# Toeplitz blocks of the FIR filters loaded as two bands of 32 columns

## The chip, the cores and the metric

One core of one Trainium2 chip. The metric is the device time of one execution in microseconds (us). The kernel before has a median of 714.42 us over 3 runs (714.11 to 716.6).

## The reference

A token mixer and a feed-forward layer over `x` of 4 x 1024 x 256, all float32. The mixer adds, per head and token, a chunked delta rule (a scan over chunks), the values `v` themselves and three causal filters along the tokens (FIR) of `v`; five gates weight them:

```
FIR_S, FIR_M, FIR_L = (3, 15, 63)
local_s = _fir(v_direct, fir_s)      # depthwise: each of the 256 channels has its own taps
local_m = _fir(v_direct, fir_m)
local_l = _fir(v_direct, fir_l)
o = probs[..., 0:1] * local_s + probs[..., 1:2] * local_m + probs[..., 2:3] * local_l
    + probs[..., 3:4] * delta_out + probs[..., 4:5] * v_direct
```

Then a norm, an output product, a layer norm, and the feed-forward part. The change touches only how the filters reach the chip.

## The kernel before, in words

The kernel runs in three stages, and each engine's program is written out in order by hand, with semaphores between engines.

**Stage A (to about 103 us)**: per batch row `b`, VectorE (DVE) takes row statistics (`a_row_stats`), normalises with `a_norm` (line 1030, a tensor_scalar from SBUF to SBUF) and does the short convolution of `v` (`a_conv`, line 1042). TensorE (PE) transposes and multiplies, ScalarE (ACT) copies out of PSUM. GpSimd (POOL) has in this stage only the small powers of `a_power` (line 487) and, behind the powers of `b` = 0 and of `b` = 1, a memset on the filter blocks (line 493). The values end in `vwin`, with 128 token offsets on the partitions.

**FIR stage (to about 177 us)**: a filter is applied as a product with a Toeplitz block: for each channel, 128 window rows by 64 output tokens. The host lays the blocks out (`padded`). Output token t of the 63-tap filter needs window rows 2+t to 64+t, that of the 15-tap filter rows 50+t to 64+t; the rest of a block is zeros. Channels come in 16 groups of 16. One group is one `load(g)` on the sync engine's DMA queue (SP): line 281 brings the long filter (`fl`), line 282 the two short ones (`fms`, rows 48 to 127 only, the rows above having been zeroed by the memset). Four buffers (NB = 4) rotate: `toep_in(g)` waits until PE is through with group g - 4 and then issues `load(g)`. Groups 0 to 3 load during stage A. Between `toep_in(5)` and `toep_in(6)` SP writes and reads back a small tensor (`beta`, lines 402 and 404), and behind `toep_in(11)` it issues the first two windows of the next stage (`window_in`, line 323, four transfers).

PE works in tiles of four channels (`fir_tile(q)`, 64 tiles, a group is four tiles). Two tiles (a pair) are 16 MATMUL records at line 1541, two at a time side by side on the two column halves, and behind each pair come two transposes of an earlier pair (line 1550). DVE multiplies each tile by the gates (line 1134), POOL adds the three filters (lines 502 and 504).

**Stage C (to the end)**: the projections (line 1611), the triangular solve on POOL (lines 571 and 573), the scan and the feed-forward part. PE's first projection stands behind its last FIR tile in program order, and its bank is free only after that.

Of the kernel before, what the change touches and what calls it, by code (L numbers as in the profile page):

```python
# [36 lines left out]
P = 128  # L37
B, L, D, H = 4, 1024, 256, 4
DK = D // H
C = 64  # L40
# [7 lines left out]
PAD = TAPS - 1  # L48
LP = L + PAD
NG = 6  # L50
MS0 = 48
ROWS = 2 * P - C

LEAD = 8
RING = LEAD + 1
# [6 lines left out]
GC = 16  # L62
NB = 4
NF = 3
TILES = D // 4
PER = GC // 4
ROW = NF * C
FPAIRS = 2
FG = D // GC
# [10 lines left out]
def build(nc, x, out, wgate, consts, smalls, wq, wk, wv, wo, wr, wfk, wfv, fl, fms):  # L80
    ctx = ExitStack()
    with ctx:
        def sb(name, shape):
            return ctx.enter_context(nc.sbuf_tensor(name, shape, F32))
# [17 lines left out]
        w = {k: sb("w_" + k, [P, HALVES, D]) for k in ("q", "k", "v", "o", "r", "fk", "fv")}  # L102
# [20 lines left out]
        A_V = BLK * D  # L123
        A_T = NB * NF * C * GC
        arena = sb("arena", [P, A_V + A_T])
        vwin = arena[:, 0:A_V].rearrange("p (c w) -> p c w", w=BLK)
        toep = arena[:, A_V:A_V + A_T].rearrange("p (i f c t) -> p i f c t", i=NB, f=NF, c=GC)

        def carve(whole, at, *shape):
            n = 1  # L130
# [34 lines left out]
        for i in range(RING):  # L165
            whole, at = (arena, low) if i < 3 else (seq, rest_) if i < EARLY else (arena, high)
            kq.append(carve(whole, at, 2 * U, C).rearrange("p (u i) t -> p u i t", i=2))
        for i in range(RING):
            whole, at = (cva.rearrange("p a t -> p (a t)"), [0]) if i == 0 else (arena, low) if i == 1 else (seq, rest_) if i < 5 else (arena, high)
# [28 lines left out]
        bank = [ctx.enter_context(nc.psum_tensor(f"bank{i}", [P, 512], F32)) for i in range(8)]  # L198
# [22 lines left out]
        HH = [slice(0, 64), slice(64, 128)]  # L221
# [26 lines left out]
        def fir_bank(q):  # L248

            return q % 4 if q < TILES // 2 else (3, 6, 7)[(q - TILES // 2) % 3]  # L250
# [9 lines left out]
        def _(sp):  # L260
# [17 lines left out]


            def load(g):  # L280
                sp.dma_start(toep[:, g % NB, 0], fl[g]).then_inc(s[f"toep{g % NB}_in"], 16)
                sp.dma_start(toep[MS0:P, g % NB, 1:3], fms[g]).then_inc(s[f"toep{g % NB}_in"], 16)


            v_dst = v_dram.rearrange("(n two) t r b k -> two t r b n k", two=2)
# [12 lines left out]
            for b in range(B):  # L298
                if b + 2 < B:
                    rows_of(b + 2, 0)  # L300
                    rows_of(b + 2, 1)
                xT_store(b)
                if b < 2:
                    sp.wait_ge(s["toep_zero"], b + 1)
                    load(2 * b)
                    load(2 * b + 1)
                v_store(b)


            def toep_in(g):  # L310
                sp.wait_ge(s["fir_mm"], (g - NB + 1) * PER)
                load(g)
# [84 lines left out]
            for pr in range(PAIRS):  # L397
                for q in range(4):
                    hh, half = divmod(q, 2)
# [76 lines left out]
        def _(pool):  # L476
# [8 lines left out]
            def a_power(b, h):  # L485
                pool.wait_ge(s["a_stats"], 6 * b + 3 * h + 3)
                pool.tensor_tensor(rs_a[:, 4 * h:4 * h + 4], ve_a[:, 4 * h:4 * h + 4], neg_half[:, 0:4], ALU.pow).then_inc(s["a_rs"], 1)

            for b in range(B):
                for h in range(2):  # L490
                    a_power(b, h)
                if b < 2:
                    pool.memset(toep[0:MS0, 2 * b:2 * b + 2, 1:NF], 0.0).then_inc(s["toep_zero"], 1)


            def fir_sum(h):
# [936 lines left out]
        def _(pe):  # L1433
            mm = nc.tensor.matmul
# [88 lines left out]
            def fir_tile(q):  # L1523

                g, pr, dp = q // PER, q // (TILES // 2), q % (TILES // 2)
                if q % PER == 0:
                    pe.wait_ge(s[f"toep{g % NB}_in"], 32 * (g // NB + 1))
                if q >= TILES // 2 + 3:
                    pe.wait_ge(s["fir_prod"], q - 2)
                elif q > TILES // 2:  # L1530
                    pe.wait_ge(s["beta_T"], PAIRS)
                elif q == TILES // 2:
                    pe.wait_ge(s["fir_prod"], TILES // 2)
                elif q >= 4:
                    pe.wait_ge(s["fir_prod"], q - 3)
                out_ = bank[fir_bank(q)][:, 0:2 * ROW].rearrange("p (f w) -> p f w", f=NF)
                for hh in range(2):
                    for i in range(2):
                        d = 2 * dp + i
                        cin = (GC // 2) * hh + d % (GC // 2)  # L1540
                        last = mm(out_[HH[i], :, 64 * hh:64 * hh + C], vwin[:, P * pr + 64 * hh + d, :],  # L1541
                                  toep[:, g % NB, :, cin, :], start=True, stop=True)
                last.then_inc(s["fir_mm"], 1)

            def fir_turn(q):
# [22 lines left out]
            for h in range(HALF_PAIRS):  # L1568
                if h == 1:
                    fir_gates(0)  # L1570
                    fir_gates(1)
                if h == 4:
                    beta_turn()
                fir_tile(2 * h)
                fir_tile(2 * h + 1)
                if h >= 2:
                    fir_turn(2 * (h - 2))
                    fir_turn(2 * (h - 2) + 1)

            def fir_tiles(n, i):  # L1580
                fir_tile(2 * late_pair(n, i))
                fir_tile(2 * late_pair(n, i) + 1)
# [353 lines left out]
```

## Time and profile before

| | |
|---|---|
| median of 3 runs | 714.42 us |
| profiled execution, its own time | 716.96 us |
| its span, first to last instruction | 715.0 us |
| mean granted TensorE clock | 0.915 |
| PE busy / DVE busy / POOL busy | 79% / 68% / 57% |
| bytes moved by DMA | 63.44 MB |
| `arena<-fl`: x16, each | 512.0 KB |
| `arena<-fms`: x16, each | 640.0 KB |

The profiled execution is 2.5 us above the median of the timed runs, and 1.96 us of it lie outside the span. A busy share is an average over three stages with different limits; what an edit is worth is read from the stage it is in.

### The profile page before, as it was taken

The numbers are of one execution on the slowest core, as the hardware profiler recorded it, in microseconds if no ns is written. First come the engines' busy times: TensorE is split into PE (matmuls) and PEld (weight loads), VectorE is DVE, ScalarE is ACT, GpSimd is POOL, SyncE is SP. The second block draws the span as 40 slices with busy tenths as digits, with TensorE's granted clock in tenths as the row PEclk, the third lists the DMA queues.
The fourth block names the chain that finished last, engine by engine and source line by source line (L and its number), as shares of the span: only waits on it lengthen the run. The fifth ranks groups of instructions, "written<-read, shape, count | busy, mean of one in ns | idle before, by whom it ended". The sixth has DMA issues, their size and how long they took to land.

```text
span 715.0 us, 20289 instructions
## 1 busy us (share of the span) xinstructions
PE 567.2 (79%) x7980; PEld 454.8 (64%) x7980; DVE 482.9 (68%) x1166; ACT 283.0 (40%) x703; POOL 406.4 (57%) x503
## 2 busy tenths in 40 slices
PE   3788769768687676578989989989867678999964
PEld 2566546545574465467877878768766567788853
DVE  6999755434646353178798796797864666788863
ACT  2688831111535244043444443634513223444421
POOL 3211018546100298548998457899649999666522
PEclk9999979999979696699999998999989898999987
DMA  8749447995112610543213243031251111422201
GB/s 279 202 137 256 154 126 195 236 224 114 31 32 56 64 47 17 92 66 74 50 25 93 54 89 71 19 86 47 68 87 31 42 46 35 84 62 57 55 15 29
DMA packets 111149, 63.44 MB, mean 89 GB/s; under 512 B 81744, under 2 KB 104144, under 8 KB 109776
## 3 DMA queue, kind: packets, MB, share of 16 engines
q1 hardware_dynamic: 111056, 62.16, 37.6%
q8 instruction: 63, 1.03, 0.6%
q14 instruction: 30, 0.25, 0.1%
HBM read 43.18 MB, written 18.95 MB: 87 GB/s over the span
## 4 chain that ended last, share of the span: by engine, by line
DVE 26%; POOL 25%; PE 17%; issue 12%; DMA 11%; SPq 7%; ACT 2%; POOLq 0%; DVEq 0%; ACTq 0%
POOL seq L573 7%; DMA arena<-fms 6%; POOL seq L571 6%; POOL arena L582 5%; DVE arena L1160 5%; DVE cva L1042 4%; DVE arena L1257 3%; SPq L367 3%; PE bank L1729 3%; PE bank L1541 2%; PE bank L1611 2%; PE bank L1645 2%; POOL arena L544 2%; POOL arena L594 2%; DVE arena L1245 2%
## 5 line engine op out<-in xcount | busy, mean ns | idle before, releaser
L1160 DVE SCALAR_TENSOR_TENSOR arena<-bank,small,arena 128x256 f32<-128x256 f32 x192 | 91.4, 482 | 25.7 <-ACT arena L816 20.8
L582 POOL TENSOR_TENSOR arena<-arena,neg_half 128x2 f32<-128x2 f32 (+1 forms) x64 | 61.5, 961 | 74.2 <-DVE arena L1252 54.3
L573 POOL TENSOR_TENSOR seq<-seq 128x31 f32<-128x31 f32 (+15 forms) x124 | 86.7, 699 | 9.7
L571 POOL TENSOR_TENSOR seq<-seq 128x31 f32<-128x31 f32 (+15 forms) x124 | 69.4, 560 | 7.9
L1541 PE MATMUL bank<-arena 128*64 128x192 f32 x512 | 51.4, 345 | 16.9 <-DMA arena<-fms 13.3
L1134 DVE TENSOR_TENSOR seq<-bank,seq 128x384 f32<-128x384 f32 x64 | 35.2, 557 | 43.4 <-PE bank L1541 33.2
L502 POOL TENSOR_TENSOR seq<-seq 128x256 f32<-128x256 f32 x32 | 23.2, 726 | 68.0 <-DVE seq L1134 63.0
L816 ACT ACTIVATE arena<-bank,small 128x256 f32<-128x256 f32 x64 | 30.4, 475 | 58.6 <-PE bank L1611 58.5
L528 POOL TENSOR_TENSOR arena<-seq,powers 128x16 f32<-128x16 f32 x16 | 47.3, 2956 | 10.7 <-DVE seq L1169 10.7
L1541 PEld LDWEIGHTS bank<-arena 128*64 128x64 f32 x512 | 35.5, 142 | 27.5 <-DMA arena<-fms 15.7
L1611 PE MATMUL bank<-arena,w_q 128*128 128x268 f32 x128 | 37.5, 429 | 15.0 <-DVE arena L1160 14.9
L1611 PE MATMUL bank<-arena,w_k 128*128 128x268 f32 x128 | 40.6, 457 | 7.1 <-DMA arena<-xnT_scratch 6.6
L1042 DVE SCALAR_TENSOR_TENSOR cva<-bank,small,cva 128x256 f32<-128x256 f32 x96 | 39.9, 476 | 6.8 <-ACT cva L695 6.5
L1257 DVE TENSOR_SCALAR arena<-arena 128x256 f32<-128x256 f32 x64 | 30.3, 514 | 16.9 <-POOL arena L582 16.9
L1611 PEld LDWEIGHTS bank<-arena,w_q 128*128 128x128 f32 x128 | 23.9, 202 | 27.5 <-DVE arena L1160 23.9
L1729 PE MATMUL bank<-w_o,arena 128*128 128x256 f32 x128 | 36.2, 432 | 1.5 <-ACT arena L870 1.4
L1729 PE MATMUL bank<-w_fv,seq 128*128 128x256 f32 x128 | 36.5, 435 | 0.8 <-ACT arena L901 0.8
L553 POOL MEMSET seq<- 128x1024 f32 x4 | 3.8, 950 | 57.8 <-DVE seq L1194 57.8
L1295 DVE SCALAR_TENSOR_TENSOR seq<-seq,small,arena 128x256 f32<-128x256 f32 x64 | 35.5, 596 | 0.3
L1611 PEld LDWEIGHTS bank<-arena,w_k 128*128 128x128 f32 x128 | 26.2, 218 | 14.8 <-DMA arena<-xnT_scratch 7.0
L1622 PE MATMUL bank<-cst,arena 64*64 64x4 f32 x1024 | 34.3, 200 | 0.2 <-DVE arena L1160 0.2
L1729 PE MATMUL bank<-w_r,seq 128*128 128x256 f32 x128 | 33.2, 404 | 1.5 <-DVE seq L1295 1.5
(159 smaller groups left out, 1422.3 us busy)
## 6 DMA issues: line engine op xcount, KB each, us to landing
arena<-fms SPq DMA_DIRECT2D x16, 640.0 KB, 13.4
arena<-fl SPq DMA_DIRECT2D x16, 512.0 KB, 10.9
arena<-xnT_scratch SPq DMA_DIRECT2D x32, 134.0 KB, 2.8
gram_scratch<-arena SPq DMA_DIRECT2D x16, 256.0 KB, 2.3
arena<-v_scratch SPq DMA_DIRECT2D x32, 128.0 KB, 3.1
arena<-x SPq DMA_DIRECT2D x64, 64.0 KB, 2.2
out<-arena SPq DMA_DIRECT2D x64, 64.0 KB, 2.1
xnT_scratch<-seq SPq DMA_DIRECT2D x2, 1027.0 KB, 8.5
```

Source lines behind the costliest of these rows:

```text
L528: pool.tensor_tensor(rk, ssel[:, slot_of(n)], powers[:, :, :], ALU.pow).then_inc(s["norms"], 1)
L571: pool.tensor_tensor(part, below, above, ALU.mult).then_inc(s["solve"], 1)
L573: last = pool.tensor_tensor(into, into, part, ALU.add)
L582: pool.tensor_tensor(dst, src, half8 if k == U else neg_half[:, 0:k], ALU.pow).then_inc(s[dst_sem], 1)
L1042: nc.vector.scalar_tensor_tensor(cva[:, i, :], bank[2 + i][:, j:j + 256], conv_w[:, 2, i, j:j + 1], cva[:, i, :], ALU.mult, ALU.add).then_ ...
L1134: nc.vector.tensor_tensor(fprod[:, q % (2 * FPAIRS), :], bank[fir_bank(q)][:, 0:2 * ROW], fgate[:, q // (TILES // 2), :], ALU.mult).then_i ...
L1160: nc.vector.scalar_tensor_tensor(cv[:, t], ps[:, :, j:j + C], conv_w[:, 1 - t // 2, t % 2, j:j + 1], cv[:, t], ALU.mult, ALU.add).then_inc ...
L1257: last = nc.vector.tensor_scalar(dst[:, j, :], src[:, j, :], mv[:, i, j, 0:1], rs[:, i, j:j + 1], ALU.subtract, ALU.mult)
L1295: nc.vector.scalar_tensor_tensor(dst[:, hf].rearrange("p (b t) -> p b t", b=B), dx[:, hf].rearrange("p (b t) -> p b t", b=B), mu[:, i, hf: ...
L1541: last = mm(out_[HH[i], :, 64 * hh:64 * hh + C], vwin[:, P * pr + 64 * hh + d, :], toep[:, g % NB, :, cin, :], start=True, stop=True)
L1611: last = mm(bank[g][:, 0:B * (C + PAD)], w["kq"[kind]][:, kh, P * g:P * g + P], xwin4[:, m % 2, kh], start=(kh == 0), stop=(kh == 1))
L1729: last = mm(dst[:, 256 * j:256 * j + 256], lhs[:, kh, P * j:P * j + P], wt[:, kh, :], start=(kh == 0), stop=(kh == 1))
```

## The change

A block of 64 columns is cut into two bands of 32 columns. Band 0 of the long filter has its taps in rows 0 to 95, band 1 in rows 32 to 127; the short ones in rows 48 to 95 and 80 to 127. Only these rows are loaded: `load(g)` has four transfers, two of 96 rows with 2 KB each (192 KB) and two of 48 rows with 4 KB each (192 KB). The memset now covers all 128 rows and all three filters of two buffers at once. In SBUF a buffer is laid out band, filter, channel, column; the matmul's moving operand is read in six runs of 32 columns in place of three of 64 (still 192), and its output access pattern puts them where they stood before.

```diff
-MS0 = 48
+BAND = C // 2
+LONG, SHORT = (0, 96), (48, 96)
...
-        toep = arena[:, A_V:A_V + A_T].rearrange("p (i f c t) -> p i f c t", i=NB, f=NF, c=GC)
+        toep = arena[:, A_V:A_V + A_T].rearrange("p (i s f c t) -> p i s f c t", i=NB, s=2, f=NF, c=GC)
...
             def load(g):
-                sp.dma_start(toep[:, g % NB, 0], fl[g]).then_inc(s[f"toep{g % NB}_in"], 16)
-                sp.dma_start(toep[MS0:P, g % NB, 1:3], fms[g]).then_inc(s[f"toep{g % NB}_in"], 16)
+                for h in range(2):
+                    sp.dma_start(toep[BAND * h + LONG[0]:BAND * h + LONG[1], g % NB, h, 0], fl[g, h]).then_inc(s[f"toep{g % NB}_in"], 16)
+                    sp.dma_start(toep[BAND * h + SHORT[0]:BAND * h + SHORT[1], g % NB, h, 1:3], fms[g, h]).then_inc(
+                        s[f"toep{g % NB}_in"], 16)
...
-                    pool.memset(toep[0:MS0, 2 * b:2 * b + 2, 1:NF], 0.0).then_inc(s["toep_zero"], 1)
+                    pool.memset(toep[:, 2 * b:2 * b + 2], 0.0).then_inc(s["toep_zero"], 1)
...
-                    pe.wait_ge(s[f"toep{g % NB}_in"], 32 * (g // NB + 1))
+                    pe.wait_ge(s[f"toep{g % NB}_in"], 64 * (g // NB + 1))
...
-                out_ = bank[fir_bank(q)][:, 0:2 * ROW].rearrange("p (f w) -> p f w", f=NF)
+                out_ = bank[fir_bank(q)][:, 0:2 * ROW].rearrange("p (f k s t) -> p k s f t", f=NF, k=2, s=2)
...
-                        last = mm(out_[HH[i], :, 64 * hh:64 * hh + C], vwin[:, P * pr + 64 * hh + d, :],
-                                  toep[:, g % NB, :, cin, :], start=True, stop=True)
+                        last = mm(out_[HH[i], hh], vwin[:, P * pr + 64 * hh + d, :],
+                                  toep[:, g % NB, :, :, cin, :], start=True, stop=True)
...
-    def padded(f):
+    def padded(f, rows_of):
...
-        return rows.reshape(ROWS, FG, GC)[at].transpose(2, 0, 3, 1)
+        whole = rows.reshape(ROWS, FG, GC)[at].transpose(2, 0, 3, 1)
+        return np.stack([whole[:, BAND * h + rows_of[0]:BAND * h + rows_of[1], :, BAND * h:BAND * h + BAND] for h in range(2)], axis=1)
...
-        "fl": padded(g["attn_fir_l"]),
-        "fms": np.stack([padded(g["attn_fir_m"]), padded(g["attn_fir_s"])], axis=2)[:, MS0:],
+        "fl": padded(g["attn_fir_l"], LONG),
+        "fms": np.stack([padded(g["attn_fir_m"], SHORT), padded(g["attn_fir_s"], SHORT)], axis=3),
```

## Rows read from the trace of the kernel before

**Rows 1.** The page's second part: busy tenths of DMA in 40 slices.
```profile
DMA  8749447995112610543213243031251111422201
```

**Rows 2.** Chain that ended last, 88 to 182 us, shares by line.
```profile
by line: DMA arena<-fms 48.6%; PE bank L1541 18.8%; DMA v_scratch<-fir 4.7%; PE bank L1550 4.1%; SPq L295 2.4%; PE bank L1466 2.4%; PE bank L1611 2.3%; issue 1.9%; DVE cva L1042 1.8%; DVE seq L1134 1.7%; DVE arena L1160 1.6%; POOL seq L502 
```

**Rows 3.** Waits, 96 to 178 us: us in total, times, longest.
```profile
PE bank L1541 <- DMA arena<-fms: 13.3, 9, 3.3
```

**Rows 4.** Timeline of PE: start us, us, what, in brackets the idle time before.
```profile
119.47 1.52 PE L1541 MATMUL bank<-arena 128*64 128x192 f32 x16
...
121.29 1.52 PE L1541 MATMUL bank<-arena 128*64 128x192 f32 x16
...
156.84 2.72 PE L1541 MATMUL bank<-arena 128*64 128x192 f32 x16 [3.31 <-DMA arena<-fms]
...
173.23 1.52 PE L1541 MATMUL bank<-arena 128*64 128x192 f32 x16
```

**Rows 5.** The same chain in order of time: start us, us, what.
```profile
118.12 12.03 DMA arena<-fms
...
153.57 17.80 DMA arena<-fms
```

**Rows 6.** Timeline of SP's DMA issues: start us, us, what.
```profile
108.23 0.43 SPq L282 DMA_DIRECT2D arena<-fms  x1
...
115.86 0.50 SPq L281 DMA_DIRECT2D arena<-fl  x1
...
127.63 0.33 SPq L281 DMA_DIRECT2D arena<-fl  x1
128.00 0.43 SPq L282 DMA_DIRECT2D arena<-fms  x1
...
134.56 10.47 SPq L323 DMA_DIRECT2D arena<-xnT_scratch  x4
145.49 3.68 SPq L281 DMA_DIRECT2D arena<-fl  x1
```

**Rows 7.** DMA issues from 108.1 to 109 us, last column us to landing.
```profile
arena<-fms SPq DMA_DIRECT2D x1, 640.0 KB, 5.7
```

**Rows 8.** The same view from 127.9 to 128.5 us.
```profile
arena<-fms SPq DMA_DIRECT2D x1, 640.0 KB, 17.4
arena<-fl SPq DMA_DIRECT2D x1, 512.0 KB, 13.9
```

**Rows 9.** Windows: stretch, length, busy of PE, PEld, DVE, ACT, POOL, clock, DMA, GB/s.
```profile
4.50:9.00 4.50, 0.00 (x0) 0.00 (x0) 3.18 (x14) 0.21 (x1) 1.02 (x1) 1.00 1.04 316
...
119.00:134.50 15.50, 11.60 (x113) 7.76 (x110) 7.38 (x14) 2.36 (x4) 9.58 (x14) 1.00 1.03 239
```

**Rows 10.** Chain that ended last, 0 to 32 us, in order of time.
```profile
10.94 3.41 issue
...
24.82 1.64 DVE seq L1030 x2
```

**Rows 11.** Timeline of POOL, 0 to 32 us.
```profile
10.68 3.60 POOL L493 MEMSET arena<- 48x4096 f32 x1
17.41 1.01 POOL L487 TENSOR_TENSOR rs_a<-ve_a,neg_half 128x4 f32<-128x4 f32 x1 [3.12 <-DVE ve_a L1022]
...
22.64 3.50 POOL L493 MEMSET arena<- 48x4096 f32 x1
```

**Rows 12.** Line 553: duration ns min/median/max, first and last start, shape.
```profile
L553 POOL MEMSET seq<- x4: 942/952/957, 245.3 to 534.5; 128x1024 f32 x4
```

**Rows 13.** Line 1030 by itself, the same columns.
```profile
L1030 DVE TENSOR_SCALAR seq<-seq,mv_a,rs_a x16: 396/408/3530, 9.5 to 49.7; 128x256 f32<-128x256 f32 x16
L1030 DVE TENSOR_SCALAR seq<-fir,mv_a,rs_a x16: 394/404/1482, 24.8 to 67.5; 128x256 f32<-128x256 f32 x16
```

**Rows 14.** Matmuls of lines 1611 (four runs of 67 columns) and 1729 (one run).
```profile
L1611 PE MATMUL bank<-arena,w_k x128: 389/389/816, 177.3 to 498.8; 128*128 128x268 f32 x128
...
L1729 PE MATMUL bank<-w_o,arena x128: 379/379/796, 320.6 to 687.7; 128*128 128x256 f32 x128
```

## The prediction

> **What bounds the kernel now.** I read four views in this order. The page's slices show where DMA is nearly full: at the start, about 50 us, and in slices 7 to 9, roughly 120 to 175 us, which is the FIR stage [rows 1]. The chain of waits there names the transfer of the short filters for 48.6% of 94 us, and PE's own tiles for only 18.8% [rows 2]. PE stops nine times for it, 13.3 us in all, 3.3 at the longest [rows 3]. The timeline gives PE's own pace: pairs start at 119.47 and 121.29, so a pair costs 1.82 us, and a group (two pairs) 3.64. That is pair 10; pair 31, the last, starts at 173.23, where 119.47 + 21 x 1.82 = 157.69 would have done. So the stage is 15.54 us longer than PE needs, which includes one pair after the longest stall that ran at a lower clock, 2.72 in place of 1.52 us [rows 4]. After the stage PE's projections follow in program order and nothing in stage C waits for a clock of its own, so what is saved here moves the end by as much.
>
> **How fast the filters come.** The chain follows two transfers to their landing: group 7 at 118.12 + 12.03 = 130.15, group 15 at 153.57 + 17.80 = 171.37 [rows 5]. Between them lie eight groups of 1152 KB and two windows (four transfers of 134 KB, 536 KB): 9752 KB in 41.22 us, 4.23 ns per KB. A group costs 4.87 us against PE's 3.64, the windows 2.27. A group that meets an empty queue landed 5.7 us after its last issue [rows 6, 7], 0.4 after the first (two issues follow each other so, 127.63 and 128.00 [rows 6]): 6.1, of which 6.1 - 4.87 = 1.2 is fixed.
>
> **Part 1, fewer bytes.** 2 x 192 + 2 x 192 = 768 KB in place of 1152. By the byte a group costs 768 x 4.23 = 3.25 us, below PE's 3.64. Follow it with times as if nothing ahead had moved. Group 6 is issued at 115.86 [rows 6], held until then by the beta round trip; two more issues for group 5 lie ahead of that and add some 0.4: 116.2 + 1.2 + 3.25 = 120.7, and PE wants it at 123.11. Group 12 has six more groups and the windows ahead: 120.7 + 6 x 3.25 + 2.27 = 142.5, wanted at 119.47 + 14 x 1.82 = 144.95. Group 15: 152.2, wanted at 155.87. None is late, by 2.4 us at least, and the whole 15.5 comes back. In general group 15 lands at 119.7 + 10c, with c the time of a group, so PE waits from c = 3.62 on, and each 0.1 us on c costs 1 us.
>
> What c could be: the low end is 3.25 or less, no gain beyond the 15.5. Shorter rows do not speak against it: x in rows of 1 KB moved at 316 GB/s, the filters in rows of 4 and 8 KB at 239, at a full queue both times [rows 9]. The high end comes from group 9's followers: the long filter of group 10 landed at 127.63 + 13.9 = 141.5, the short ones at 128.00 + 17.4 = 145.4 [rows 6, 8]. That is 3.9 us for 640 KB in rows 48 to 127, so 6.1 ns per KB, while the long filter over all 128 rows had at most the remaining 1 us or so of that group's 4.87, 2 ns per KB. A transfer that sits mostly in the upper 64 rows is slow, or an engine of the queue has more of it. Bounded that way, the two short pieces (rows 48 to 95 and 80 to 127, all but 16 of 96 rows in the upper half) cost 192 x 6.1 = 1.17 each, 2.3 together; the two long ones (each two to one between the halves) cost between 0.8 and 2.3 together. So c is 3.1 to 4.65. Summed over the halves it is 256 KB below and 512 above, before 384 and 768: the same two to one, so if the pieces overlap, c is two thirds of 4.87 again. I take 3.25 to 3.7 as likely and charge 0.6 us for it.
>
> The Trainium skill bears on this: "SBUF — State Buffer", section on the DMA port swizzle, says a DMA's bandwidth goes by how many of 16 ports its partitions reach, partitions 0 to 63 all on eight of them and 64 to 127 on the other eight, and the section after it that two DMAs on the two halves do not add up. By its figure of 218 GB/s for eight ports the four pieces one after another would take about 0.6 + 0.6 + 0.6 + 0.9 = 2.7 us, an estimate from that page. The rate of 6.1 ns per KB above is in line with its direction, not with its size. Its direction makes the second rival below.
>
> **Part 2, SP's issues.** 32 more, 0.33 to 0.43 us each [rows 6], 1.7 us per group where a group has 3.64: hidden. In the middle SP stood 10.47 us at the windows and 3.68 at the next filter, since the queue was backed up [rows 6]. With the backlog gone by then to one or two groups, that wait ends when the windows begin to move, about 137, and group 12 is still issued in time. If it is not, group 12 is late by some 2 us; part of the 0.6 charge is for this.
>
> **Part 3, the larger memset.** Each memset grows from 4096 to 6144 elements per partition. POOL's two took 3.60 and 3.50 us with 48 partitions [rows 11]; one of 1024 elements on 128 took 0.95 [rows 12], so the slope is (3.55 - 0.95) / 3072 = 0.85 ns per element whatever the partitions, and each grows by 2048 x 0.85 = 1.74 us. POOL itself has the room (its next instruction is at 17.41 after 3.12 us idle [rows 11]), and SP's filter loads come later. But DVE does not. Its normalisation (line 1030) needs 0.4 us, and took 3.53 once and 1.48 once [rows 13]: the chain stands still for 3.41 us from 10.94, and for 1.64 at 24.82 for two of them [rows 10], in both cases until the memset is over (10.68 + 3.60 = 14.28; 22.64 + 3.50 = 26.14) [rows 11]. DVE is the chain there and runs on without a gap, so the first memset delays everything by 1.74. The second then starts as much later, meets the same instruction, and delays by 1.74 again. Together 3.5 us, on the path, since from there to the FIR stage DVE, ACT and PE wait only for one another. The ends: 0 if the wait were not for the memset, 3.5 if it is; two instructions that end with it make it 3.5.
>
> **Part 4, the matmul's pattern.** 192 columns as before, in six runs. Between four runs of 67 columns and one of 256 the median differs by 389 - 379 = 10 ns for 12 more columns [rows 14], 0.83 ns per column and nothing for the three added runs. At most the 10 ns are all runs: 10 ns on 8 steps of a pair, 30 pairs, 2.4 us. A gain is excluded, since columns are the same. I take 0.
>
> **Sum.** -15.5 + 0.6 + 3.5 = -11.4 us. The profiled span would be 703.6 and its execution 705.6; on the median of 714.4 that is 703.0. What is late next: in the FIR stage PE itself, at 1.82 us a pair.
>
> **Rivals.**
> A (forecast, 0.62): c up to 3.7, memset on the path: 702 to 704.5.
> B (0.17): the pieces cost more than the bytes say, c = 3.7 to 4.4, or SP's wait at the windows starves group 12. At c = 4.0 group 15 lands at 159.7, 3.8 us late: 714.4 - 15.5 + 3.8 + 3.5 = 706.2; at 4.4 it is 710. For it: the slow short filters [rows 8]. Against: the same two to one over the halves.
> C (other side, 0.07): transfers that cover half the height do not overlap, and all four run at 6.1 ns per KB: c = 768 x 6.1 = 4.7. Then the ten groups from 6 on save only 10 x (4.87 - 4.7) = 1.7 us, the memsets take 3.5: 716.2, slower. It decides from 10 x (4.87 - c) = 3.5, c about 4.5. Against it: it needs the long pieces, a third of whose rows are in the other half, to be as slow as the short ones.
> D (0.08): the longer memset does not hold DVE longer: 699.5. Against it: rows 10, 11 and 13 agree to 0.2 us.
> E (0.06): the change does its work, but matmuls in six runs or a lower clock in the denser stage cost 2 to 5 us: 705 to 708.
>
> **How the numbers follow.** Range 699.5 to 709: D and E in full, B but for its upper end, C left out. Below 0.5% (3.6 us), about what this kernel's runs can tell from nothing, lie only C and the last of B: faster 0.88, same 0.05, slower 0.07.
>
> **What would show it.** Both memsets at about 5.3 us, line 1030's longest instructions at about 5.3 and 3.2 us, and pair 10 starting at 123 in place of 119.47. Pairs every 1.82 us from there to the last, which starts near 161; no wait of line 1541 for `fms` over 1 us; SP's stall at the windows much shorter than 10.47. Landing times of a group's last piece below 10 us in the place of 17.4. The prediction is wrong if pairs come at over 1.85 us with no wait in between (part 4), if line 1541 still waits in every group (C), or if the FIR stage begins where it began (D).

## The result, and the profile after

| | kernel before | changed kernel |
|---|---|---|
| median of 17 executions | 717.57 us (714.02 to 1287.64) | 709.45 us (703.88 to 714.3) |
| ratio, 95% interval | | 0.9895 (0.986 to 0.993) |
| profiled execution, span | 715.0 us | 701.9 us |
| bytes moved | 63.44 MB | 57.15 MB |

The ratios here and below compare means over the executions that lie within 1.5% of the fastest of their kernel, which leaves out the one of 1287.64 us, and on the chip of memsets_moved_2 and both_moved_2 leaves only 8 of the 17 of the kernel before (mean 713.5 us, that of all 17 is 718.5).

By the ratio the kernel is faster by 7.5 us (5.0 to 10.0) where 11.4 was forecast, and 709.45 lies just outside the range that ended at 709. The single profiled execution, though, gained 13.1 us of span; it was the fastest of its 17. So there are two questions: did the steps go as worked out, and why do executions and profile differ?

The chain of waits from 88 to 182 us, shares by line, answers to [rows 2]:

```profile
by line: PE bank L1544 47.9%; PE bank L1553 11.7%; DMA v_scratch<-fir 5.2%; PE bank L1614 4.0%; DVE arena L1163 3.7%; PE bank L1648 3.1%; DVE gates L1101 2.5%; SPq L298 2.4%; PE bank L1469 2.4%; issue 2.3%; PE bank L1625 2.2%; DVE seq L1137
```

No filter transfer is left in it; PE's own tiles (line 1544, before 1541) are 47.9%. The timeline of PE, answering to [rows 4] (first the pairs 2 and 3, then 10, 15, 16 and 31):

```profile
108.21 2.15 PE L1544 MATMUL bank<-arena 128*64 128x192 f32 x16 [3.34 <-DVE seq L1137]
...
110.91 2.22 PE L1544 MATMUL bank<-arena 128*64 128x192 f32 x16
...
124.77 1.52 PE L1544 MATMUL bank<-arena 128*64 128x192 f32 x16
...
133.87 1.52 PE L1544 MATMUL bank<-arena 128*64 128x192 f32 x16
...
136.15 1.52 PE L1544 MATMUL bank<-arena 128*64 128x192 f32 x16 [0.38 <-DVE seq L1137]
...
163.45 1.52 PE L1544 MATMUL bank<-arena 128*64 128x192 f32 x16
```

Pairs come every 1.82 us in six runs as they did in three. Two things are new: pair 16 waits for DVE (its bank is the one that pair 15 used; before, the DMA wait covered that), and pairs 2 and 3 ran at a lower clock, 2.15 us in place of 1.52 (from 108.21 to 113.70 us the granted clock was 0.69).

Stage A: the chain from 0 to 32 us, POOL's memsets, and line 1033 (before 1030) by itself, answering to [rows 10, 11, 13]:

```profile
11.02 5.12 issue
...
27.59 1.68 DVE seq L1033
29.27 0.45 issue
```

```profile
10.76 5.31 POOL L496 MEMSET arena<- 128x6144 f32 x1
...
24.43 5.22 POOL L496 MEMSET arena<- 128x6144 f32 x1
```

```profile
L1033 DVE TENSOR_SCALAR seq<-seq,mv_a,rs_a x16: 394/406/5236, 9.5 to 53.2; 128x256 f32<-128x256 f32 x16
L1033 DVE TENSOR_SCALAR seq<-fir,mv_a,rs_a x16: 395/407/2203, 27.6 to 71.3; 128x256 f32<-128x256 f32 x16
```

The memsets take 5.31 and 5.22 us (5.3 forecast) and DVE is held for 5.12 in place of 3.41. The longest instruction of the first form is 5.24 us as forecast, that of the second 2.20 where 3.2 was.

How fast the filters come, at a full queue: SP's issues of the last pieces of groups 7, 11, 12, 13 and 15 at line 284, then their landing times in the same order, from the DMA issues at each of these times:

```profile
125.11 0.41 SPq L284 DMA_DIRECT2D arena<-fms  x1
...
136.72 1.46 SPq L284 DMA_DIRECT2D arena<-fms  x1
...
145.25 0.43 SPq L284 DMA_DIRECT2D arena<-fms  x1
...
147.13 0.43 SPq L284 DMA_DIRECT2D arena<-fms  x1
...
151.97 0.43 SPq L284 DMA_DIRECT2D arena<-fms  x1
```

```profile
arena<-fms SPq DMA_DIRECT2D x1, 192.0 KB, 5.6
...
arena<-fms SPq DMA_DIRECT2D x1, 192.0 KB, 7.9
...
arena<-fms SPq DMA_DIRECT2D x1, 192.0 KB, 5.4
...
arena<-fms SPq DMA_DIRECT2D x1, 192.0 KB, 6.8
...
arena<-fms SPq DMA_DIRECT2D x1, 192.0 KB, 8.1
```

Group 7 landed at 130.7 and group 11 at 144.6, so c was (144.6 - 130.7) / 4 = 3.5 us there. Behind the windows group 12 landed at 150.65, group 13 at 153.9 and group 15 at 160.1: c = (160.1 - 153.9) / 2 = 3.1 us, with the last group, which has nothing behind it, in the mean. 3.25 was forecast and 4.87 measured before. SP's stop at the windows is shorter (four issues 2.59 us in place of 10.47), the one at group 12 is not (3.26 us against 3.68):

```profile
138.38 2.59 SPq L326 DMA_DIRECT2D arena<-xnT_scratch  x4
141.01 3.26 SPq L283 DMA_DIRECT2D arena<-fl  x1
```

### The profile page after: what moved, and what is told of

Read it like the earlier page. It is cut to its first block, busy times and chain, and to the rows that moved or that the text cites. A ratio compares the mean times of both kernels' runs of the same rounds, so it can differ in the third digit from the quotient of the medians.

```text
span 701.9 us, 20321 instructions
## 1 busy us (share of the span) xinstructions
PE 572.8 (82%) x7980; PEld 458.1 (65%) x7980; DVE 486.5 (69%) x1166; ACT 282.6 (40%) x703; POOL 410.4 (58%) x503
## 2 busy tenths in 40 slices
DMA packets 112941, 57.15 MB, mean 81 GB/s; under 512 B 82256, under 2 KB 104656, under 8 KB 112848
## 4 chain that ended last, share of the span: by engine, by line
DVE 27%; POOL 25%; PE 24%; issue 13%; DMA 4%; SPq 4%; ACT 2%; POOLq 0%; DVEq 0%; ACTq 0%
POOL seq L576 7%; PE bank L1544 6%; DVE arena L1163 6%; POOL seq L574 6%; POOL arena L585 5%; DVE cva L1045 4%; PE bank L1732 4%; DVE arena L1260 3%; PE bank L1614 3%; PE bank L1648 2%; POOL arena L547 2%; SPq L370 2%; DVE seq L1298 2%; PE bank L1625 2%; PE bank L1457 2%
## 5 line engine op out<-in xcount | busy, mean ns | idle before, releaser
L505 POOL TENSOR_TENSOR seq<-seq 128x256 f32<-128x256 f32 x32 | 23.3, 729 | 54.3 <-DVE seq L1137 54.2
L1614 PE MATMUL bank<-arena,w_k 128*128 128x268 f32 x128 | 43.3, 482 | 6.5 <-DMA arena<-xnT_scratch 5.1
L1614 PEld LDWEIGHTS bank<-arena,w_k 128*128 128x128 f32 x128 | 27.8, 232 | 14.9 <-DMA arena<-xnT_scratch 5.5
L1625 PEld LDWEIGHTS bank<-cst,arena 64*64 64x64 f32 x1024 | 34.3, 145 | 1.9 <-issue 1.4
```

What stands on the lines that cost most here:

```text
L1614: last = mm(bank[g][:, 0:B * (C + PAD)], w["kq"[kind]][:, kh, P * g:P * g + P], xwin4[:, m % 2, kh], start=(kh == 0), stop=(kh == 1))
L1625: last = mm(bank[1][q, NONE * (U * kind + u):NONE * (U * kind + u) + NONE], sq[q, U * kind + u], ones[q], start=True, stop=True)
```

## The experiments

They ran with 6 or 12 timed executions each, on three chips, beside 17 of the kernel before on the same chip. Stage times come from one profile each: "FIR" is from the start of pair 2 to that of pair 31 in PE's timeline, "gap" from pair 31 to the first memset of the solve, the first work of POOL in stage C.

| kernel | ratio (95%) | pair 0 | FIR | pair 31 | gap | span |
|---|---|---|---|---|---|---|
| before, first profile | | 95.65 | 69.28 | 173.23 | 72.1 | 715.0 |
| changed, first profile | 0.9895 (0.986-0.993) | 99.44 | 55.24 | 163.45 | 69.5 | 701.9 |
| after_again | 0.9866 (0.9819-0.9912) | 99.10 | 54.55 | 161.86 | 76.7 | 709.9 |
| after_third | 0.9815 (0.9748-0.9882) | 99.48 | 56.15 | 163.93 | 64.6 | 699.9 |
| windows_last | 0.9845 (0.9797-0.9892) | 99.67 | 55.23 | 164.42 | 69.0 | 705.1 |
| before_big_memset | 1.0059 (1.0017-1.0101) | 99.80 | 69.66 | 177.67 | 68.3 | 715.5 |
| before_memsets_moved | 0.9839 (0.977-0.9908) | 91.59 | 68.76 | 168.66 | 65.8 | 704.5 |
| memsets_moved | 0.9795 (0.974-0.9851) | 92.55 | 58.01 | 158.73 | 70.7 | 702.1 |
| memsets_moved_2 | 0.9889 (0.9818-0.996) | 93.21 | 54.73 | 156.18 | 74.8 | 703.6 |
| both_moved | 0.9727 (0.9666-0.9789) | 93.14 | 56.48 | 159.31 | 67.5 | 694.0 |
| both_moved_2 | 0.9838 (0.9785-0.9891) | 92.75 | 54.19 | 156.54 | 68.5 | 695.7 |

**after_again, after_third**: the changed kernel, unedited.

> The changed kernel once more, unedited. Its first profiled execution gained 13.1 us of span (715.0 to 701.9), its 17 executions only about 1% (7.5 us) in the mean. Theory W (windows): group 12 landed at 145.25 + 5.4 = 150.65 us there and pair 24 started at about 150.7, so there was no room at all; in many executions PE waits there. Expected by W: a profile whose pairs 24 to 31 start 1 to 4 us later than 1.82 us a pair would have it, with the wait on fms. Theory C (stage C): the FIR stage is always as in the first profile, 60.0 us from pair 2's start to the last pair's end of its tiles within 1 us, and the spread lies behind it, where the kernel before has it too. Expected by C: no wait on fms, and a length from the last pair to the end that differs by 2 us or more from the 538.4 us of the first profile.

> The changed kernel, unedited, on this chip. From the positions of the last FIR pair (173.2 before, 163.5 and 161.9 in the two profiles of the changed kernel) its gain should be about 10.5 us, a ratio of 0.985 to 0.986. Theory N: 0.985 once enough executions are pooled. Theory D: 0.989, since 2 to 3 us are given back behind the FIR stage in every execution.

Both theories of the first expectation (W: PE waits for group 12; C: the spread lies behind the FIR stage) got a part. The FIR stage is the same within 1.6 us in the three profiles, but after_again needed 548.0 us behind pair 31 where the first profile needed 538.5: 9.6 us for the same program. 7.2 of it lie in the gap, and there the windows view (from PE's first projection to the first solve) shows PE's clock, first the first profile, then after_again:

```profile
167.52:232.96 65.44, 46.82 (x566) 36.14 (x565) 34.83 (x79) 28.64 (x70) 3.12 (x2) 0.89 0.27 42
```

```profile
165.92:238.59 72.67, 55.99 (x565) 43.66 (x564) 35.03 (x79) 28.65 (x70) 3.12 (x3) 0.77 0.25 38
```

The columns are those of [rows 9]. The work is the same (DVE 34.83 and 35.03 us, ACT 28.64 and 28.65), PE needs 46.82 or 55.99 us for it, at a mean granted clock of 0.89 or 0.77. So the first profile of the changed kernel was on the fast side. The ratio of after_third, 0.9815 (0.9748 to 0.9882), holds the 0.985 of its theory N and just leaves out the 0.989 of its theory D, that the denser FIR stage costs clock behind it. Pooling the three ratios of the changed kernel by their intervals gives 0.9874 +/- 0.0026, which is 9.0 +/- 1.9 us of 717.6.

**before_again**: the null.

> The kernel before, unedited, for a second profile of its stages and as a null. Ratio 1.00. Stage C from the last FIR pair to the end took 541.8 us in its first profile; in four profiles of kernels with the same stage C it took 537.8 to 548.0, and nearly all of the difference lay between the last FIR pair and the first solve, 68 to 77 us, by the granted clock. Theory N (noise of the clock): this profile differs from the first by up to 5 us there, with the FIR stage within 1 us of the first. Theory D (the denser FIR stage lowers the clock behind it): this profile again has 68 to 72 us from the last pair to the first solve.

Ratio 1.002 (0.997 to 1.007), median 721.98. Its profile took 730.54 us, the longest of its 12 executions, and is not in the table; its FIR stage was 69.95 us (pair 31 at 174.70) and its gap 76.3. An execution that is that long as a whole doesn't decide between the theories N (only noise) and D. Over the other profiles the gap is 72.1, 68.3 and 65.8 us with the slow FIR stage and 64.6 to 76.7, mean 70.2, in eight with the dense one: the 1.4 us between the means are well inside the scatter of 3 to 4. That the denser stage costs clock behind it is neither shown nor excluded; so few profiles would not show a difference under some 5 us.

**before_big_memset**: the memset's size alone.

```diff
-                    pool.memset(toep[0:MS0, 2 * b:2 * b + 2, 1:NF], 0.0).then_inc(s["toep_zero"], 1)
+                    pool.memset(toep[:, 2 * b:2 * b + 2], 0.0).then_inc(s["toep_zero"], 1)
```

> The kernel before with nothing changed but the memset's size, 128 x 6144 in place of 48 x 4096. By part 3 of the prediction stage A is 3.5 us longer. What the whole loses: theory 1, all 3.5 us, since the FIR stage then starts later and takes as long as before. Theory 2: less, since in the kernel before the FIR stage waits for DMA, and a part of the loads (groups 4 to 6) hangs on stage A only by the first PE tiles, so all move alike and nothing is absorbed; then again 3.5. Rival D: 0. Expected 717.9 where the kernel before has 714.4, a ratio of 1.005.

Ratio 1.0059, which is 4.2 us (1.2 to 7.3), and pair 0 starts 4.15 us later than in the kernel before, 99.80 for 95.65 (0.35 of it is older than the first memset, which starts at 11.03 for 10.68). Its chain holds the same line as the changed kernel's:

```profile
11.28 5.12 issue
```

With the full-height loads the FIR stage is as long as before, 69.66 us. Part 3 holds, and rival D is out.

**before_memsets_moved** and **memsets_moved**, **memsets_moved_2**: the memsets where DVE is not held, with the old and with the new loads. The edit is shown on the changed kernel; in the kernel before the moved memsets keep their 48 rows.

```diff
+            pool.memset(toep[:, 0:2], 0.0).then_inc(s["toep_zero"], 1)
             for b in range(B):
                 for h in range(2):
                     a_power(b, h)
-                if b < 2:
-                    pool.memset(toep[:, 2 * b:2 * b + 2], 0.0).then_inc(s["toep_zero"], 1)
+                if b == 1:
+                    pool.wait_ge(s["a_normed"], 16)
+                    pool.memset(toep[:, 2:4], 0.0).then_inc(s["toep_zero"], 1)
```

> The kernel before with its two small memsets moved to where DVE is not held (ahead of the first power, and behind all normalisations of row 1). By part 3 of the prediction the held time is 3.41 + 1.07 = 4.5 us: 709.9 where the kernel before has 714.4, a ratio of 0.9937. If the memset did not hold DVE: 1.00. The FIR stage stays DMA-bound with its 15 us of waits.

> The changed kernel with its first memset moved ahead of the first power (POOL is idle from 1.1 to 6.5 us and it takes 5.3) and its second one behind all of row 1's normalisations (POOL then has 32.4 to 36.8 free, and the power behind it is not needed before 43). If the memset is what holds DVE's line of normalisations: 3.41 + 1.74 = 5.15 and 1.07 + 1.74 = 2.8 us go, 8.0 together, and the first FIR pair starts 8 us sooner; the longest of these instructions is then about 0.4 us. If only the added part of the memset matters or DVE is held by something else (rival D): 0 to 3.5 us. Expected 8 us faster than the changed kernel, so about 2.1% faster than the kernel before.

> The changed kernel with its memsets moved, once more, beside the next one. Its gain on the kernel before was 13.2 us in the means (0.9795); from the terms (10.4 for the changed kernel, 8.0 for the memsets) it should be 18, less some 2 for PE's wait on group 12: a ratio of 0.977 to 0.979. Its profile should again show a wait of line 1546 for fms at the pair of group 12, 0.3 to 2.5 us.

In the old kernel pair 0 starts 4.06 us sooner (4.5 expected) and pair 31 4.57; the ratio 0.9839 says 6.6 to 16.5 us, which leaves out the 4.5, and its profile has the second shortest gap of the table, 65.8 us. What the memsets are worth is taken from the stages; the rest of that ratio is open. In the changed kernel pair 0 starts 6.9 and 6.2 us sooner than in its first profile (8.0 expected; where the other 1.1 and 1.8 went isn't shown), and line 1030's counterpart has no long one left (memsets_moved, line 1035):

```profile
L1035 DVE TENSOR_SCALAR seq<-seq,mv_a,rs_a x16: 402/406/417, 9.6 to 46.5; 128x256 f32<-128x256 f32 x16
L1035 DVE TENSOR_SCALAR seq<-fir,mv_a,rs_a x16: 404/408/414, 22.4 to 64.4; 128x256 f32<-128x256 f32 x16
```

**windows_last**, **both_moved**, **both_moved_2**: the first two windows behind the last filter loads; in the latter two with the memsets moved as well.

```diff
-            window_in(0)
-            window_in(1)
...
                     toep_late(n + 6)
+                if n + 6 == FIRST + 3:
+                    window_in(0)
+                    window_in(1)
```

> The changed kernel with the first two windows issued behind the filter loads of groups 12 to 15, not ahead of them. SP's stop at group 12 (3.26 us) and the 2.3 us of window traffic ahead of group 12 go. Theory W: 1 to 4 us faster than the changed kernel in the mean, and a narrower spread. Theory C: the same within 1 us, since PE did not wait for fms in the profile; the group 12 lands some 4 us before PE wants it. A cost could show if the windows now land after the last pair: at 3.1 us per group and 2.3 for the windows they land near 162, PE wants them at 167.5.

> The changed kernel with its memsets moved and its two windows behind the last filter loads: the version the runs so far point to. Against the kernel before: 10.5 us from the loads, 4.5 from the memsets (8.0 against the changed kernel), and the 2.3 us wait of PE for group 12 that the profile with moved memsets showed (140.35 to 144.51 in place of 142.17, and low-clock after it) gone: 695.5 to 698, a ratio of 0.975 to 0.978. Theory W: no wait on fms at all, and a faster median than the kernel with the memsets moved alone (0.9795). Against it: no difference between the two.

> The same with the windows behind the last filter loads, on the same chip as the run beside it. Theory W (SP's stop at the windows starves group 12): no wait for fms in the profile, and 1 to 3 us faster than its neighbour, a ratio of 0.974 to 0.976. Theory N (only the clock's noise): the same ratio as its neighbour.

In the first profile of the changed kernel group 12 landed 0.06 us before pair 24. In others it was late, by up to 2.3 us. Timeline of PE, pair 24 of after_third and of memsets_moved:

```profile
150.71 1.52 PE L1544 MATMUL bank<-arena 128*64 128x192 f32 x16 [1.41 <-DMA arena<-fms]
```

```profile
144.51 2.83 PE L1546 MATMUL bank<-arena 128*64 128x192 f32 x16 [2.27 <-DMA arena<-fms]
```

after_again has 0.29 there and memsets_moved_2 0.46. In memsets_moved the wait was followed by a pair at the lower clock, 2.83 us for 1.52, at a granted clock of 0.50. In windows_last, both_moved and both_moved_2 PE waits for no filter at all. So theory W's mechanism is shown: four of five profiles with the windows first have the wait, none of three with the windows last. From pair 10 to pair 31, which leaves out the changing clock of pairs 2 and 3, the three with the windows last need 38.67 us each and the five others 38.68 to 42.49, 40.0 in the mean. So the order is worth 0 to 3.8 us, 1.3 in the mean. It shows no price further on: up to 240 us PE waits for a window at most once, behind 220 us, for 2.7 to 3.8 us with the windows last and for 0 to 5.3 with them first.

The timed executions are too coarse to show this. On the same chips 0.9845 stands beside 0.9866 and 0.9838 beside 0.9889, 1.5 and 3.7 us in the expected direction with intervals that overlap. The narrower spread that theory W wanted did not show: 704.4 to 713.1 us in windows_last, 707.1 to 712.0 in after_again. The mean of the whole FIR stage is 55.3 beside 55.7 in the profiles; it hides the difference, since both_moved had pairs 2 and 3 at a granted clock of 0.55.

The two ratios on the third chip missed what was expected of them, 0.9889 for 0.977 to 0.979 and 0.9838 for 0.974 to 0.976. Both rest on the low mean of 713.5 us there.

both_moved is the fastest kernel, 0.9727 and 0.9838 on two chips (intervals that barely meet; pooled the same way 0.979 +/- 0.004, 15 us), some 6 us more than the changed kernel's 9.

## Why the prediction was right and wrong

**The step that failed** is the last one of the sum, "on the median of 714.4 that is 703.0". The 714.4 was the median of three executions. Sets of 17 executions put the kernel before at 717.57, 718.94, 719.2 and 718.92, and 3.2 of the 6.5 us between 703.0 and 709.45 come from that alone: on 717.57 the same range would have been 702.7 to 712.2. Executions of the changed kernel alone spread from 702 to 714 us, with two more at 715 and 719, so the spread is wider than the whole range of 699.5 to 709. A mean clock of 0.915 said that the clock changes; three executions within 2.5 us of each other did not say how often. The number also fell among those of rival B (706 to 710), but not for B's reason: c was not 3.7 to 4.4.

**The size.** The other 3.3 us are the gain, 8.1 us between the two medians (7.5 by the ratio) in place of 11.4. With the two later sets the ratio gives 9.0 +/- 1.9, and pair 31, which carries no noise of stage C, moved from 173.23 to 163.45, 161.86 and 163.93: 10.2 us in the mean, against one profile of the kernel before. The term of the sum that was mis-sized is part 1. Of the 1.2 us between 10.2 and 11.4 it makes 0.9, part 3 makes 0.2, and 0.1 lies between pairs 0 and 2:
- *Part 1, -15.5 + 0.6.* 14.0, 14.7 and 13.1 us measured from pair 2 to pair 31, mean 14.0 for 14.9. "None is late, by 2.4 us at least, and the whole 15.5 comes back" failed. In the first profile the 1.5 us that lack are accounted for: 0.46 at pair 16, a wait for DVE that the DMA wait had covered (the prediction said that PE itself is late next and missed it), and 1.04 for pairs 2 and 3 at the lower clock. In after_third it is pair 16 again and the waits for groups 12 and 13 (1.41 and 0.41).
- *c.* 3.1 to 3.5 us for 3.25 (before, 4.9 over the same groups 7 to 11); rival C, at 4.7, is out, and so is the milder B from 3.7 on: the pieces, with 512 of 768 KB in the upper half, kept the rate per byte to within some 10%.
- *Part 2, SP's issues.* Hidden as said, but for group 12. "That wait ends when the windows begin to move, about 137" missed: SP stood until 144.3 in the profile, group 12 came at 150.65 against 142.5 worked out (146 with the stage's shift of 3.5), and the forecast's margin of 2.4 us was none. Not all of that is SP's stop: group 6 landed at 127.3 where 120.7 + 3.5 = 124.2 was worked out, and from there to group 12 it took 23.3 us where 21.8 was.
- *Part 3, +3.5.* 3.8, 3.4 and 3.8 at pair 0, 4.15 with the memset alone. Mechanism and size hold, and so do the two parts of 1.74: from the start of the first memset to the end of the second it is 15.46 us before (10.68 to 26.14) and 18.89 after (10.76 to 29.65), 3.43 more. That the second hold grew by 0.72 only (1.48 to 2.20 us) is no contradiction, below.
- *Part 4.* 0, as taken: pairs come every 1.82 us in both kernels. That takes the first half of rival E out; its second, a lower clock behind the denser stage, is open.

The Trainium skill's port rule ("SBUF — State Buffer", on the DMA port swizzle), which had spoken against half-height transfers, is neither borne out nor refuted here: the estimate made from it was 2.7 us per group, below the 3.1 to 3.5 measured, so the rule, in these numbers, is not what set the time. What would have decided it is a kernel with the pieces in other partitions, and that was not run.

One reading of the prediction was off without consequence: slices 7 to 9 of [rows 1] are 107 to 161 us, not 120 to 175.

What stays open: the 17 executions gained 7.5 us and pair 31 moved 10.2. The pooled 9.0 +/- 1.9 covers both, so nothing has to be missing; a systematic loss of up to some 3 us behind the FIR stage can't be excluded.

## What to carry to other kernels

Before a memset or another long POOL instruction is made larger, look at what DVE does beside it: here two instructions of 0.4 us each were held to the memset's end, and moving the memsets started the FIR stage 6 to 7 us sooner in the changed kernel, whose whole gain was 9. When a DMA bound goes away, walk the consumer's other waits and the queue's order once more: the next late thing was a small transfer of another stage standing ahead of the wanted one. And take the base of a forecast from many executions, or give the range the spread that a changing clock makes.

## What the runs showed that was not expected

After a long hold of DVE PE ran at a lower clock, and the next hold hid it. After the 5.12 us hold PE, which had been idle for 3.33 us, ran its next product at half the clock. PE timeline and windows of the changed kernel, then the same product's window in memsets_moved:

```profile
21.22 3.79 PE L1457 MATMUL bank<-seq,w_v 128*128 128x259 f32 x8 [3.33 <-DVE cva L1045]
```

```profile
21.20:25.10 3.90, 3.88 (x12) 2.67 (x16) 2.61 (x11) 1.64 (x5) 1.63 (x2) 0.50 0.48 183
```

```profile
17.80:19.90 2.10, 2.06 (x12) 1.57 (x16) 2.03 (x10) 2.02 (x6) 0.00 (x0) 1.00 0.10 32
```

A granted clock of 0.50 is 1.2 GHz, 1.00 is 2.4. The product took 3.3 to 3.8 us in all five profiles with the large memset in its old place and 1.99 in all five with the memset moved. With the small one in its old place it was 2.80 in the first profile, after 2.77 us of idle time, and 1.99 in before_again, after 2.56. That the idle time lowered the clock is argued from this order, and not shown by a run of its own.

On the path it cost nothing. From the start of the first memset to the end of the second it is 18.89 us in all five profiles with the large one, and 15.46 and 15.47 in the two with the small one, whatever the product took: the second memset holds DVE to its own end, and where the product is shorter, that hold is longer. Product and longest held instruction in before_again and in after_again:

```profile
19.07 1.99 PE L1454 MATMUL bank<-seq,w_v 128*128 128x259 f32 x8 [2.56 <-DVE cva L1042]
```

```profile
L1030 DVE TENSOR_SCALAR seq<-fir,mv_a,rs_a x16: 395/407/2296, 23.6 to 67.1; 128x256 f32<-128x256 f32 x16
```

```profile
20.84 3.31 PE L1457 MATMUL bank<-seq,w_v 128*128 128x259 f32 x8 [3.33 <-DVE cva L1045]
```

```profile
L1033 DVE TENSOR_SCALAR seq<-fir,mv_a,rs_a x16: 395/408/2687, 26.7 to 70.9; 128x256 f32<-128x256 f32 x16
```

The sums are 1.99 + 2.30 = 4.29 us, beside 2.80 + 1.48 = 4.28 in the first profile of the kernel before, and 3.31 + 2.69 = 6.00, beside 3.79 + 2.20 = 5.99 in that of the changed one. So product and second hold together grew by 1.7 us, as the memset did.

The other thing is the size of the clock's noise: in one and the same program 64.6, 69.5 and 76.7 us between the last FIR pair and the first solve.
